# Products with one column of weights in front, early rows turned two steps later, and two splits moved ahead

## The reference

```python
q, k, v = heads(x @ q_w.T + q_b), ...               # 16 heads of 32
qp, kp = elu(q) + 1, elu(k) + 1
kv = einsum('bhsd,bhse->bhde', kp, v)               # linear attention, not causal
z = einsum('bhsd,bhd->bhs', qp, kp.sum(axis=2))
attn = einsum('bhsd,bhde->bhse', qp, kv) / (z + 1e-6)
x = x + attn_joined @ o_w.T + o_b
...
gates = softmax(ln(x) @ gating_w); top_k(gates, 2)  # 8 experts, each takes at most 1280 rows
h = relu(rows_of_expert @ w1[e] + b1[e])            # 512 -> 2048
y = h @ w2[e] + b2[e]                               # 2048 -> 512
x = x + (weighted rows of the two chosen experts)
```

## Time and profile before

| | |
|---|---|
| median of three executions | 2056.42 us |
| the profiled execution | 2061.28 us, span 2059.7 us |
| TensorE busy | 2006.3 us (97%) |
| VectorE, ScalarE, GpSimd busy | 903.2, 628.7, 431.0 us |
| mean granted TensorE clock | 0.991 |

### The profile page before, as it was taken

One profiled execution on the slowest core, in us unless ns is written; L12 is line 12 of the kernel. 1 busy time (PEld: TensorE's weight loads), 2 busy tenths in 40 slices (PEclk: granted clock), 3 DMA queues, 4 the chain that ended last, 5 costly groups with the idle time before them and its releaser, 6 DMA issues.

```text
span 2059.7 us, 29934 instructions
## 1 busy us (share of the span) xinstructions
PE 2006.3 (97%) x10620; PEld 1776.0 (86%) x10621; DVE 903.2 (44%) x1730; ACT 628.7 (31%) x981; POOL 431.0 (21%) x545
## 2 busy tenths in 40 slices
PE   9999999997999989999999999999999999999996
PEld 8889999987889989998998788889988988988895
DVE  4445666656633443245323422443235244334332
ACT  3433334334322332134212312232124124123221
POOL 1012225154621121122112011021121120120221
PEclk9999999999999999999999999999999999999998
DMA  5312122235321531054104312331043143142221
GB/s 140 115 36 75 65 83 78 62 106 182 93 42 25 164 83 20 20 145 104 18 24 113 103 35 51 111 88 20 20 122 103 25 112 100 37 108 95 46 41 20
DMA packets 115407, 156.12 MB, mean 76 GB/s; under 512 B 28560, under 2 KB 61456, under 8 KB 115344
## 3 DMA queue, kind: packets, MB, share of 16 engines
q1 hardware_dynamic: 93744, 112.13, 17.4%
q0 software_dynamic: 21600, 43.16, 11.4%
HBM read 113.16 MB, written 42.10 MB: 75 GB/s over the span
## 4 chain that ended last, share of the span: by engine, by line
PE 88%; issue 4%; POOL 3%; DVE 2%; ACT 2%; DMA 1%; POOLq 0%; ACTq 0%; DVEq 0%
PE bank L1423 16%; PE bank L1425 16%; PE bank L1424 16%; PE pair_v L1423 7%; PE pair_v L1425 7%; PE pair_v L1424 7%; PE pair_o L1425 4%; PE pair_o L1424 4%; PE pair_o L1423 4%; POOL slot_table L585 2%; PE bank L1431 1%; PE pair_v L1442 1%; PE bank L1409 1%; PE bank L1547 1%; PE pair_o L1442 1%
## 5 line engine op out<-in xcount | busy, mean ns | idle before, releaser
L980 DVE CAST h_hi<-h 128x512 fp32r<-128x512 f32 x320 | 139.2, 435 | 849.8 <-ACT h L733 849.7
L570 POOL DMA_INDIRECT out_dram<-ys,tab_s x80 | 129.1, 1614 | 1029.3 <-ACT ys L720 1011.0
L1423 PE MATMUL bank<-w_hi,h_hi 128*128 128x512 f32 x752 | 296.4, 394 | 1.4 <-DVE w_lo L960 1.4
L1425 PE MATMUL bank<-w_hi,h_lo 128*128 128x512 f32 x752 | 295.0, 392 | 0.0
L1424 PE MATMUL bank<-w_lo,h_hi 128*128 128x512 f32 x752 | 295.0, 392 | 0.0
L733 ACT ACTIVATE h<-pair_v,b_cur 128x512 f32<-128x512 f32 x160 | 110.1, 688 | 509.9 <-PE pair_v L1425 509.9
L733 ACT ACTIVATE h<-bank,b_cur 128x512 f32<-128x512 f32 x160 | 109.8, 686 | 486.7 <-PE bank L1425 482.2
L1423 PE MATMUL bank<-et_hi,w_hi 128*128 128x384 f32 (+1 forms) x640 | 229.3, 358 | 14.4 <-issue 8.7
L1425 PE MATMUL bank<-et_hi,w_lo 128*128 128x384 f32 (+1 forms) x640 | 228.1, 356 | 0.0
L1425 PE MATMUL pair_v<-et_hi,w_lo 128*128 128x384 f32 (+1 forms) x640 | 227.8, 356 | 0.0
L1423 PE MATMUL pair_v<-et_hi,w_hi 128*128 128x384 f32 (+1 forms) x640 | 227.6, 356 | 0.0
(11 more groups left out here) (259 smaller groups left out, 3563.4 us busy)
## 6 DMA issues: line engine op xcount, KB each, us to landing
w_raw<-L_ffn_w_dram SPq DMA_DIRECT2D x128, 512.0 KB, 3.6
xb<-_attn_hidden_states_dram SPq DMA_DIRECT2D x32, 256.0 KB, 2.7
xr<-_attn_hidden_states_dram SPq DMA_DIRECT2D x32, 256.0 KB, 3.1
out_dram<-x SPq DMA_DIRECT2D x32, 256.0 KB, 3.5
normed<-x1n SPq DMA_DIRECT2D x32, 256.0 KB, 3.8
normed<-zrow SPq DMA_DIRECT2D x1, 2048.0 KB, 8.1
out_dram<-zrow SPq DMA_DIRECT2D x1, 2048.0 KB, 14.2
b_cur<-L_ffn_b_dram SPq DMA_DIRECT2D x8, 256.0 KB, 4.1
```

Source lines behind the costliest of these rows:

```text
L570: nc.gpsimd.indirect_dma_start(out=out, out_offset=bass.IndirectOffsetOnAxis(ap=tab_s[:, h, 0:1].bitcast(I32), axis=0), in_=ys[:, h, :], i ...
L980: ve_.tensor_copy(h_hi[:, mm % 4, :], h32[:, mm % 2, :]).then_inc(h_split_hi, 1)
L1423: mm_(out_, lh, rh, start=(first and c == 0), stop=False, skip_group_check=shared)
L1425: ins = mm_(out_, ll, rh, start=False, stop=(last and c == n - 1), skip_group_check=shared)
```

## The change

- `warm` takes `cols` columns of the ones as weights too, not just as the moving side, so `warm(n, 1)` has one column of weights and writes one number. The first call runs 14 products in place of 22. The call ahead of the loop is `warm(7, 1)` in place of `warm(6, 1)`. The calls `warm(2)`, `warm(6)` are unaltered; `warm(6, 1)` in step 3 keeps its count and has one column of weights.
- `EARLY_TURN` moves pieces 0 and 1 from step 40 to 42, and pieces 2 and 3 from step 42 to 44, on TensorE, ScalarE and VectorE alike.
- `EARLY_NEXT` is 14 in place of 13.
- On ScalarE the wait for `o_full` and `w2_split(0, 0)` stand ahead of `variance_x1(31)` and `normalize_x1(31)`. On VectorE `w2_lo_part(0, 0)` stands ahead of `route_logits(3)`.

```diff
-        EARLY_TURN = {EARLY_TABLE + 3: (0, 1), EARLY_TABLE + 5: (2, 3)}
+        EARLY_TURN = {EARLY_TABLE + 5: (0, 1), EARLY_TABLE + 7: (2, 3)}
...
-        EARLY_NEXT = 13
+        EARLY_NEXT = 14
...
             normalize_x1(NTILES - 2)
+            act.wait_ge(o_full, NTILES)
+            w2_split(0, 0)
             variance_x1(NTILES - 1)
             normalize_x1(NTILES - 1)
-            act.wait_ge(o_full, NTILES)
-            w2_split(0, 0)
             early_weights(0)
...
             hidden(0, 0)
+            w2_lo_part(0, 0)
             route_logits(B - 1)
-            w2_lo_part(0, 0)
             early_weights(0)
...
             def warm(times, cols=P):
 
                 for _ in range(times):
-                    mm_(bank[6][:, 0:cols], ones[:], ones[:, 0:cols], start=True, stop=True)
+                    mm_(bank[6][0:cols, 0:cols], ones[:, 0:cols], ones[:, 0:cols], start=True, stop=True)
 
             pe.wait_ge(ones_set, 1)
-            warm(22, 1)
+            warm(14, 1)
...
             warm(2)
-            warm(6, 1)
+            warm(7, 1)
```

## The result

| | before | after |
|---|---|---|
| median (six executions each) | 2057.34 us | 2048.88 us |
| range | 2055.88 to 2059.12 | 2047.18 to 2049.51 |
| profiled execution, span | 2061.28, 2059.7 us | 2048.14, 2046.5 us |
| TensorE busy | 2006.3 us | 1990.3 us |

The ratio is 0.9957, 95% interval 0.9945 to 0.997: 8.5 us faster in medians. The traces are read for where the time went, the medians for how much it is.

The account below looks back on a forecast made before the run. TensorE was taken as the bound, 88% of the chain that ended last. Front 8.1, early rows 0, splits 1.35 and EARLY_NEXT 0.8 sum to 10.3 us off 2056.4, giving 2046.1 us, range 2043 to 2051.5.

Parts of the forecast that it names:

- The front: Kernel start: narrow ones let turning begin at 6.3 us and the first v product at 11.6; 8.1 us gained.
- Rival 1: At the start, narrow weights cost what wide ones do: only 2.9 us gained, 2051.3 us; chance 0.10.
- the clock: First products at the start: a later rise from half rate could cost up to 1.7 us; 0.6 us taken.
- Rival 3: At the start, the clock rises no sooner than 23.7 us: 6.8 us gained, some 2049.6 us; chance 0.06.
- The early rows: Steps 40 to 44: turning pieces two steps later gains 0 us, bounds 0.5 us gained to 0.9 lost.
- Rivals 2 and 5: Moved rows late for step 45 or uncovered at 42, 2047.4 us, 0.08; half clock after step 41's idle, 2063 us, 0.03.
- The splits and EARLY_NEXT: End of the steps and second tile's gather: splits moved ahead gain 1.35 us, turning next rows later adds 0.8 us.
- The sum: Whole kernel: 8.1 + 0 + 1.35 + 0.8 = 10.3 us gained, from 2056.4 to 2046.1 us; chance 0.68.

Follow-up runs that it names:

- width_only: The kernel before with only the weights of the ones cut to one column, counts 22, 2, 6 kept: 2052.31 us, ratio 0.9967.
- count_only: The kernel before with only the counts of the ones changed to 14, 2, 7, weights still 128 columns: 2057.04 us, ratio 0.9986.
- after_again: The changed kernel run a second time, beside the kernel before on one chip: 2048.44 us, ratio 0.9946.
- after_third: The changed kernel run a third time, beside the kernel before on one chip: 2048.08 us, ratio 0.9951.
- before_again: The kernel before, unedited, run again for a second trace; median in its job 2059.59 us.
- turn_only: The kernel before with only the early rows turned two steps later: 2065.54 us against 2064.70, ratio 1.0003.
- late_only: The kernel before with only both splits moved ahead and EARLY_NEXT at 14: 2063.03 us against 2064.70, ratio 0.9985.
- splits_only: The kernel before with only the two splits moved ahead, EARLY_NEXT left at 13: 2064.81 us against 2059.77, ratio 1.0024.
- front_only: The kernel before with only the three edits of the products of ones: 2058.90 us against 2064.70, ratio 0.9974.
- spread: The changed kernel with GpSimd's four early-row gathers moved behind the root VectorE awaits, table copy one step later: 2047.84 us, ratio 0.9922 to the kernel before.
- spread_again: The same kernel as spread, run again beside the changed kernel on one chip: 2040.04 us, ratio 0.9906 to the kernel before.
- no_ones: The changed kernel without any products of ones: 2050.81 us, ratio 0.9961 to the kernel before.

## Why the prediction was right

**The front.** Right in mechanism and nearly in each time: turning 6.32 us (said 6.3), ScalarE's wait 5.19 (5), first v product 11.46 (11.6), narrow records 0.030 us each (under 0.09). Rival 1 is out by width_only against count_only. The mis-sized term is the clock: 0.6 us of loss was taken against the kernel before, and in the traces there was a gain. It had risen by the time the products began. The end of the first k product was 9.4 us ahead in the first pair, 9.0 in after_again and 10.6 in after_third against before_again, where 8.1 was said. Rival 3 is out.

How far this depends on the execution is seen when all traces with the old front are set beside all with the new one (us; when the granted clock was first at 2.4 GHz, and the end of the first k product):

| front | clock up | first k product done |
|---|---|---|
| old: before, turn_only, late_only, before_again, splits_only | 23.6, 26.4, 26.0, 26.2, 18.5 | 28.07, 29.34, 29.14, 29.27, 25.71 |
| new: after, front_only, spread, after_again, spread_again, after_third | 10.7, 9.9, 10.1, 10.0, 9.4, 10.1 | 18.64, 19.71, 20.20, 20.24, 19.46, 18.66 |

In four of the six with the new front the clock fell back to one half near 13 us for 3.4 us; in after and after_third it stayed up. The means are 28.3 and 19.5, 8.8 us apart, and single pairs give 5.5 to 10.7. In splits_only the clock was up before the old front's first product (19.38 us), so the sentence that the ones had not raised it holds for four of the five.

Two figures of this part of the prediction don't follow from its rows. It lets a narrow record take 0.13 us before the first product moves, but that leaves out the second group of ones: turning would end at 9.0, and 12 wide and 12 narrow records of 0.13 take 4.1 us more, to 13.1, where the product is due at 11.6. Worked out with both groups the limit is about 0.10. And rival 3 starts from a front of 9.0 us where the paragraphs before it have 8.7. Neither mattered at 0.030 us.

**The early rows.** The step said zero, that the gather only names the idle and VectorE's wait for the root holds it, and both came as said: turn_only 1.0003, one idle of 9.22 us (9.6 said) ended by the attention rows, pieces 2 and 3 inside the next wait, which shrank from 1.35 to 0.59 us. `spread` and `spread_again` show the cause by taking it away. Rivals 2 and 5 did not come: no idle at step 45, and the half rate in this place lasts 10.2 us in the traces of before and of after alike.

**The splits and EARLY_NEXT.** Together 2.15 us were said. In the traces the two waits went with what surrounds them, 1.5 and 1.2 us; late_only gained 1.7 in medians, 3.1 by the ratio. Right as a sum. What failed in size is what EARLY_NEXT guards against: the prediction had it that GpSimd's list would take back 1.35 us at s = 13. splits_only shows 6.1 us instead, made of a wait longer by 3.6 and half-rate work behind it. The direction, that this edit is needed beside the other, was right. The prediction counted the split's 1.23 us on VectorE as free, since it filled a wait there; that the scatters beside it would run 1.9 us longer was not in it.

**The sum.** 10.3 us said, 8.5 measured first, 11.1 and 11.7 in two jobs on chip 5. The median is 2.8 us above the forecast of 2046.1, and 0.9 of that is the base: the three executions that it was taken from had a lower median than all six. The edits alone give 5.8 + 1.7 - 0.8 = 6.7 us in medians on chip 14, and the whole 11.1 on chip 5; with intervals of about 2 us on each part that does not contradict, and it does not show that parts add. They need not: front_only keeps EARLY_NEXT at 13, and loses 1.3 us at the gather that the whole change does not wait for. Some luck is in the nearness of 8.5 to 10.3: the traced pair gained 13.1, and the front alone varies from one pair of traces to another by 5 us. Why it is near 9 us in most traces and 5.8 to 7.3 in medians is open in part. One of five traces with the old front had its first k product some 3 us before the others, with the clock up sooner; how often that happens in the executions without a trace is not on record.

## What to carry to other kernels

When an engine idles on a transfer, look at what the instruction behind it would have waited for: here the wait named was of 5 us, moving it gave nothing, and moving four DMA issues on GpSimd's list behind one short operation gave 8. An edit that lets one engine arrive sooner at a rendezvous that another sets is worth nothing or less until the rendezvous is moved as well. Products that only pass the time should have the smallest weights that do it, and end before the data comes; it was not shown here that they are needed at all (no_ones).

## What the runs showed of the hardware

- A float32 record with one moving column took 0.216 us with 128 columns of weights and 0.030 us with one, both at 1.2 GHz by the spacing of the products of full width behind them. The Trainium skill (TensorE: Matmul & The Clock Gate, Step-by-step: what each phase is for) has the time of a weight load go with its column count; by these rows it goes down with it, to a seventh and not to a 128th.
- Indirect DMAs of GpSimd took 0.97 us on their own engine in most rows of the scatters, and 1.4 to 2.0 in some, with the same shape. 32 of them together took 49.2 us in all eight traces with the moved splits, and 47.3 to 48.6 in the six without; what sets the length of a single one is open.
- TensorE was busy with ones from 1.5 to 14.5 us in the old front, and the granted clock was first at 2.4 GHz at 23.6 to 26.4 us in four traces and at 18.5 in the fifth.
- At the gather of the second tile a wait of 4.4 us of TensorE went with 6.8 us at half rate (splits_only) and one of 2.7 with 3.4 us (count_only); one of 2.8 (front_only) and those of 0.5 to 1.5 did not.
